# The last slot and the last units on VectorE: low codes, products, weighing and the closing sum, with the last four units in four PSUM banks

## The chip, the cores and the metric

One core of a Trainium2 chip. The metric is the device time in microseconds of one execution of the whole program; the time given for the kernel before is the median of 3 runs.

The engines are called by the names of the profile: PE (TensorE), ACT (ScalarE), DVE (VectorE), POOL (GpSimd), and SP, whose queue issues most DMAs.

## What is computed

16 images of 96x96 with 77 text tokens each become 16 x 113 = 1808 tokens of 192 features. One attention layer follows, and then a mixture-of-experts layer in which all 16 experts work on every token, each on a selection of half the features:

```python
pe = softmax(posembed @ pos_w + pos_b)
y = moe_mlp(hidden, sg_w, su_w, sd_w)                      # shared, 384 wide
for i in range(16):
    gate_feature = hidden * pe[i] @ gate_w + gate_b
    gate_weight, gate_idx = top_k(gate_feature, 96)        # of 192
    gate_weight = softmax(gate_weight)
    gathered = take_along_axis(hidden, gate_idx, axis=-1)
    y = y + moe_mlp(gathered * gate_weight, eg_w[i], eu_w[i], ed_w[i])
yn = (y - mean(y)) * rsqrt(var(y) + 1e-6) * ln_g + ln_b
return silu(yn @ m1_w + m1_b) @ m2_w + m2_b                # + hidden before the norm
# moe_mlp(x, g, u, d) = silu(x @ g) * (x @ u) @ d
```

## The kernel before, in words

**Tiles and slots.** The tokens are one rest tile of 16 and 14 tiles of 128. A tile's 16 experts go in 4 groups of 4; a group of a tile is a block, and every engine's program is a row of `slot`s, one per block, 57 in all (numbers 0 to `LAST` = 56). VectorE's slot is the top-k search (`max`, `max_index`, `match_replace`, lines 620 to 626), 12 rounds for each of 4 experts, and then the digits of the indices (lines 600 and 601).

**The gather.** It is done by matmuls, 8 tokens (an octet) at a time, 16 octets in a slot. An index is split into a high and a low digit. For octet o, `make_code` on PE (line 1144) writes two banks, `CODE_B` and `CODE_B + 1`, of 384 columns: where the digit is met, the value is 1, and elsewhere 0 or less. ACT's `code_out` (line 745) copies both with a Relu to `code`. `look` (line 1154) multiplies the high code with a table of the tokens' features into `LOOK_B`, one of two banks. ACT's `looked_up` (line 753) copies that to SBUF, and POOL multiplies it with the low code to `picked` (line 995). `put` (line 1164) sums `picked` for every 4 octets into the bank `XG_B`. ACT's `scale_out` (line 807) scales it with `einv` to `xs`, and POOL's `weigh` (line 963) multiplies it with the exponentials `ew` to `xw`. PE's `turn_x` (line 1173) transposes it, ACT's `turned_out` (line 719) copies it to `xwt`.

**The units.** A unit is one expert (or half of the shared layer) on one tile. `up` on PE (line 1207, 8 matmuls) writes gate and up features into the one bank `GU_B`. ACT's `activate` writes tanh of half the gate (line 793) and a copy of the bank (line 794). POOL's `hide` makes three products and sums (lines 930, 933, 936), and `down` (line 1227, 4 matmuls) adds into the bank `Y_B`. An `up` waits until ACT has read the unit before.

**The order.** It is written by hand in tables of steps, 16 steps to a slot, the same steps on all engines (`UNIT_SPOTS`, `GATE_SPOTS`, `TAIL_SPOTS`, `DOWN_LAG`, `TURN`, `FINAL_*`). In each step ACT, POOL and PE do the octet and then `step_work(step)`: a unit at its spot, its `down` 4 steps later, the turn of the block before at step 3, pieces of the next images' attention. ACT's `prepare(n + 1)` at step 8 of slot n waits for VectorE's search of the block n + 1, so that these engines run behind VectorE. Block 56's four units have the spots 5, 7, 9, 11 of the steps behind the last slot (`AFTER` and on), and the last tile's end follows.

**A tile's end.** ACT copies `Y_B` to `y` with its sum (line 815), takes the squares (line 822), POOL the mean and the power (lines 1002 to 1009), ACT normalises (line 825). PE turns it (line 1236), ACT scales and shifts (line 829), PE the first layer (line 1242), ACT adds the bias (line 835) and takes tanh of half (line 839), POOL a product and a sum (lines 1012, 1014), PE the second layer (line 1248), ACT halves it into `m2s` (line 844), POOL adds `resid` (line 1019) and issues the store to `out` (line 1021) from its own queue.

Of the kernel before, what the change touches and what calls it, by code (L numbers as in the profile page):

```python
# [189 lines left out]
GATE_AT = gate_steps()  # L190
TURN_AT = {OCT * (n + 1) + TURN: n for n in range(LAST + 1)}
FINAL_PE_AT, FINAL_ACT_AT, FINAL_POOL_AT = final_steps(FINAL_PE), final_steps(FINAL_ACT), final_steps(FINAL_POOL)

# [52 lines left out]
def build(nc, patches, txt, w_patch, b_patch, w_qk, scale, w_v, w_o, pos_t, w_pos, w_gate, b_gate, w_shared,  # L246
# [7 lines left out]
    with ExitStack() as ctx:  # L254
# [128 lines left out]
        m1_done, st1_ready, m2_done, fin_ready = sem("m1_done"), sem("st1_ready"), sem("m2_done"), sem("fin_ready")  # L383
        out_done = sem("out_done")

# [21 lines left out]
        with nc.Block() as block:  # L407

            @block.sync
            def _(sp):  # L410
# [127 lines left out]
                sp.wait_ge(late_in, LATE)  # L538
                sp.wait_ge(out_done, 16 * TILES + 16)

            @block.vector
            def _(dve):
# [99 lines left out]
                slots(slot)  # L642

            @block.scalar
            def _(act):
# [93 lines left out]
                def code_out(n, o):  # L739

                    act.wait_ge(code_done, OCT * n + o + 1)
                    if n or o >= 4:
                        act.wait_ge(picked_ready, OCT * n + o - 3)
                    w = experts_of(n) * TOP
                    nc.scalar.activation(code[:, o % 4, :, 0:w], ps[:, CODE_B:CODE_B + 2, 0:w], ACT.Relu).then_inc(code_ready, 1)  # L745

# [29 lines left out]
                def slot(t, g):  # L776
                    n = block_no(t, g)
                    for o in range(OCT):
                        looked_up(n, o)
# [107 lines left out]
                slots(slot)  # L887
                for step in range(AFTER, AFTER + 2 * OCT + 2):
                    step_work(step)

            @block.gpsimd
            def _(pool):
# [95 lines left out]
                def slot(t, g):  # L988
                    n = block_no(t, g)
                    w = slice(0, experts_of(n) * TOP)  # L990
                    for o in range(OCT):
                        pool.wait_ge(looked_out, OCT * n + o + 1)
# [43 lines left out]
                slots(slot)  # L1036
                for step in range(AFTER, AFTER + 2 * OCT + 2):
                    step_work(step)

            @block.tensor  # L1040
            def _(pe):
# [105 lines left out]
                def look(n, o):  # L1147
# [3 lines left out]
                    pe.wait_ge(code_ready, OCT * n + o + 1)  # L1151
                    if n or o >= 2:
                        pe.wait_ge(looked_out, OCT * n + o - 1)
# [3 lines left out]
                def put(n, r):  # L1157

                    if r == 0 and n:
                        pe.wait_ge(scaled, n)  # L1160
                    pe.wait_ge(picked_ready, OCT * n + QUADS * (r + 1))
                    w = slice(0, experts_of(n) * TOP)
# [12 lines left out]

                def up(tm, u, e, half):
                    rest_tile = tm == 0
# [13 lines left out]
                    pe.wait_ge(gu_out, GU_NTH["unit", tm, u] - 1)  # L1191
                    for a in range(2):
                        for c in range(2):
                            wide = REST if rest_tile and e is None else TILE
                            at = a * D + c * HALF
                            dst = ps[0:HALF, GU_B, (2 * a + c) * TILE:(2 * a + c) * TILE + wide]
                            if e is None:
# [13 lines left out]
                def down(tm, u, e, half):  # L1211
# [4 lines left out]
                    last_u = (REST_UNITS if rest_tile else UNITS) - 1  # L1216
                    many = PACK if e == "band" else 1
                    for x in range(many):
                        for c in range(2):
# [7 lines left out]
                            ins = nc.tensor.matmul(ps[0:REST if rest_tile else TILE, Y_B, 0:D], hid[:, u % 2, c, own], w,  # L1227
                                                   start=(u == 0 and x == 0 and c == 0), stop=(u == last_u and x == many - 1 and c == 1))
# [77 lines left out]
                slots(slot)  # L1306
                for step in range(AFTER, AFTER + 2 * OCT + 2):
                    step_work(step)

# [70 lines left out]
```

## Time and profile before

| | |
|---|---|
| median of 3 runs | 2670.26 us |
| lowest, highest | 2662.3, 2677.62 us |
| the profiled execution | 2661.93 us |
| its span | 2660.1 us |
| VectorE, PE, POOL, ACT busy | 94%, 85%, 67%, 64% of the span |
| mean granted TensorE clock | 0.906 |

The profile shows one execution, in microseconds from the start of the span. PE is TensorE's matmuls, PEld its weight loads. A granted clock of 1.00 is 2.4 GHz, of 0.50 is 1.2 GHz.

### The profile page before, as it was taken

The page shows a single profiled execution, that of the slowest core. Times are in us where ns is not written, and L with a number is a line of the kernel's source. Part 1 is how long each engine was busy: PE and PEld are TensorE (multiplying, and loading weights), DVE is VectorE, ACT ScalarE, POOL GpSimd, SP SyncE. Part 2 cuts the span into 40 slices and gives each one's busy share as a digit, 9 for nine tenths or more (in the row PEclk, how much of TensorE's full clock was granted, in tenths as well). Part 3 has the DMA queues.
Part 4 walks back from the last instruction along what each step waited for, and adds up shares of the span by engine and source line. Part 5 has one row for each costly group of instructions (what it writes and reads, how often), then busy time and mean ns, then how long its engine had stood idle before and what let it go on. Part 6 is the DMA issues. An engine that isn't in the chain of part 4 may idle for free.

```text
span 2660.1 us, 48026 instructions
## 1 busy us (share of the span) xinstructions
PE 2264.7 (85%) x11466; PEld 1232.5 (46%) x11466; DVE 2488.9 (94%) x13377; ACT 1703.8 (64%) x3995; POOL 1773.8 (67%) x2142
## 2 busy tenths in 40 slices
PE   4478998888889889898988988989899888897886
PEld 3345544444454454454544544445445443353444
DVE  3699799999999999999999999999999999999960
ACT  2243776767676667577675767667666666666664
POOL 1133878677677676677766777768677676676766
PEclk8587999999998989899898999899989898889877
DMA  2211222222222222122221222222122122221220
GB/s 61 54 31 39 52 53 59 49 55 51 46 59 53 51 53 52 49 53 52 52 52 44 58 45 55 56 49 62 45 54 50 40 58 52 52 53 45 49 49 16
DMA packets 124750, 133.67 MB, mean 50 GB/s; under 512 B 39931, under 2 KB 112598, under 8 KB 124462
## 3 DMA queue, kind: packets, MB, share of 16 engines
q1 hardware_dynamic: 122996, 127.82, 20.6%
q8 instruction: 95, 1.56, 0.2%
q0 software_dynamic: 928, 1.72, 0.2%
q14 instruction: 185, 1.52, 0.2%
q10 hardware_dynamic: 546, 1.06, 0.1%
HBM read 102.77 MB, written 27.87 MB: 49 GB/s over the span
## 4 chain that ended last, share of the span: by engine, by line
DVE 84%; PE 7%; DMA 3%; issue 2%; ACT 2%; POOL 1%; SPq 1%; ACTq 0%; POOLq 0%; DVEq 0%
DVE idx L624 30%; DVE keys L626 28%; DVE vals L620 24%; PE ps L1154 1%; PE ps L1227 1%; DMA looked_s<-in_mask_in 1%; DMA digit_d<-dcode 1%; DVE nmax L580 1%; SPq L465 1%; PE ps L1204 1%; DMA rows<-digit_d 1%; DVE ntop L596 1%; PE ps L1207 1%; DVE digits L601 0%; PE ps L1078 0%
## 5 line engine op out<-in xcount | busy, mean ns | idle before, releaser
L995 POOL TENSOR_TENSOR picked<-looked_s,code 128x384 f32<-128x384 f32 (+1 forms) x912 | 896.1, 991 | 479.0 <-ACT looked_s L753 477.2
L624 DVE FIND_INDEX8 idx<-vals,keys 128x8 uint16<-128x192 f32 x2712 | 939.8, 347 | 0.0
L753 ACT ACTIVATE looked_s<-ps 128x384 f32<-128x384 f32 (+1 forms) x912 | 447.8, 491 | 630.2 <-PE ps L1154 628.1
L620 DVE MAX8 vals<-keys 128x8 f32<-128x192 f32 x2712 | 820.3, 342 | 30.7 <-ACT keys L712 30.7
L626 DVE MATCH_REPLACE8 keys<-vals,keys 128x192 f32<-128x192 f32 x2486 | 839.9, 338 | 0.0
L1154 PE MATMUL ps<-code,table 128*128 128x384 f32 (+1 forms) x1824 | 832.5, 540 | 0.0
L745 ACT ACTIVATE code<-ps 128x768 f32<-128x768 f32 (+1 forms) x912 | 738.0, 809 | 59.2 <-PE ps L1144 52.0
L1144 PE MATMUL ps<-rows,codew 17*128 17x384 bf16 (+1 forms) x1824 | 317.8, 345 | 217.0 <-ACT code L745 155.5
L1144 PEld LDWEIGHTS ps<-rows,codew 17*128 17x128 bf16 x1824 | 86.6, 91 | 767.8 <-ACT code L745 416.4
L1154 PEld LDWEIGHTS ps<-code,table 128*128 128x128 f32 x1824 | 309.4, 202 | 201.1 <-issue 166.1
L1207 PE MATMUL ps<-xwt,wexp 96*96 96x128 f32 x1792 | 270.4, 298 | 37.4 <-ACT xwt L719 32.9
L1207 PEld LDWEIGHTS ps<-xwt,wexp 96*96 96x96 f32 x1792 | 219.5, 174 | 103.8 <-ACT xwt L719 46.6
L1164 PE MATMUL ps<-picked,place 128*32 128x384 f32 (+1 forms) x1824 | 217.3, 552 | 25.7 <-POOL picked L995 25.7
L930 POOL TENSOR_TENSOR prod_s<-gu_s 96x256 f32<-96x256 f32 x256 | 184.6, 721 | 80.8 <-ACT gu_s L794 79.4
L1227 PE MATMUL ps<-wdown,hid 96*128 96x192 f32 (+1 forms) x960 | 220.6, 357 | 1.9 <-POOL hid L936 1.8
L1122 PE MATMUL ps<-wgate,nt_gate 96*128 96x384 f32 x448 | 188.2, 546 | 14.6 <-DMA nt_gate<-normt_d 11.5
L933 POOL TENSOR_TENSOR turned_s<-prod_s,tanh_s 96x256 f32<-96x256 f32 x256 | 184.5, 721 | 20.1
L936 POOL TENSOR_TENSOR hid<-prod_s,turned_s 96x256 f32<-96x256 f32 x256 | 184.1, 719 | 20.0
L624 DVE MATCH_VALUE_LOAD idx<-vals,keys 128x8 f32 x2712 | 195.4, 72 | 0.0
L955 POOL TENSOR_TENSOR dcode<-dcode 128x768 bf16<-128x768 bf16 (+1 forms) x57 | 82.9, 1454 | 167.5 <-ACT dcode L727 167.5
L1227 PEld LDWEIGHTS ps<-wdown,hid 96*128 96x128 f32 (+1 forms) x960 | 159.1, 194 | 43.2 <-issue 27.9
L626 DVE MATCH_VALUE_LOAD keys<-vals,keys 128x8 f32 x2486 | 166.9, 67 | 0.0
(145 smaller groups left out, 2212.1 us busy)
## 6 DMA issues: line engine op xcount, KB each, us to landing
wexp<-in_w_exp SPq DMA_DIRECT2D x58, 576.0 KB, 4.4
wdown<-in_w_down SPq DMA_DIRECT2D x58, 576.0 KB, 4.4
digit_d<-dcode SPq DMA_DIRECT2D x56, 384.0 KB, 2.6
rows<-digit_d SPq DMA_DIRECT2D x224, 96.0 KB
table<-norm_d SPq DMA_DIRECT2D x448, 3.0 KB
patch<-in_patches SPq DMA_DIRECT2D x16, 108.0 KB, 4.9
tok_d<-h SPq DMA_DIRECT2D x16, 84.8 KB
norm_d<-hs SPq DMA_DIRECT2D x16, 84.8 KB
```

Source lines behind the costliest of these rows:

```text
L620: nc.vector.max(vals[:, par, e, at], from_keys[:, e, :]).then_inc(chain, 1)
L624: found = nc.vector.max_index(idx[:, par, e, at], vals[:, par, e, at], from_keys[:, e, :])
L626: nc.vector.match_replace(from_keys[:, e, :], vals[:, par, e, at], from_keys[:, e, :], NEG).then_inc(chain, 1)
L745: nc.scalar.activation(code[:, o % 4, :, 0:w], ps[:, CODE_B:CODE_B + 2, 0:w], ACT.Relu).then_inc(code_ready, 1)
L753: nc.scalar.activation(looked_s[:, o % 4, 0:w], ps[:, LOOK_B[o % 2], 0:w], ACT.Copy).then_inc(looked_out, 1)
L995: nc.gpsimd.tensor_tensor(picked[:, o % PICKS, w], looked_s[:, o % 4, w], code[:, o % 4, 1, w], ALU.mult).then_inc(picked_ready, 1)
L1122: ins = nc.tensor.matmul(ps[:, bank, 0:2 * D], nt_gate[0:HALF + k, k, :], wgate[0:HALF + k, k, GRP * g + 2 * pair:GRP * g + 2 * pair + 2, ...
L1144: ins = nc.tensor.matmul(ps[:, CODE_B + a, w], codew[at, :], rows[at, octet(o), w], start=True, stop=True)
L1154: ins = nc.tensor.matmul(ps[:, LOOK_B[o % 2], w], table[:, o, :], code[:, o % 4, 0, w], start=True, stop=True)
L1164: ins = nc.tensor.matmul(ps[32 * q:32 * (q + 1), XG_B, w], place[:, r, :], picked[:, (QUADS * r + q) % PICKS, w], start=(r == 0), stop=(r ...
L1207: ins = nc.tensor.matmul(dst, wexp[:, e // GRP % 2, e % GRP, at:at + HALF], xwt[:, e % GRP, :], start=True, stop=True)
L1227: ins = nc.tensor.matmul(ps[0:REST if rest_tile else TILE, Y_B, 0:D], hid[:, u % 2, c, own], w, start=(u == 0 and x == 0 and c == 0), stop ...
```

## The change

In the last slot and behind it VectorE, whose search is over, takes over work. The core of the diff (the added semaphores `code_low`, `picked_last`, `doubled`, `out_last` and some lines of the same kind left out):

```diff
+LAST_UNITS = [UNIT_AT[AFTER + spot] for spot in TAIL_SPOTS]
+LAST_BANKS = [GU_B, CODE_B, CODE_B + 1, LOOK_B[0]]
...
# sync
-                sp.wait_ge(out_done, 16 * TILES + 16)
+                sp.wait_ge(fin_ready, TILES + 1)
+                sp.dma_start(out[start(TILES):start(TILES) + TILE, :], fin[:]).then_inc(out_last, 16)
+                sp.wait_ge(out_done, 16 * TILES)
+                sp.wait_ge(out_last, 16)
...
# vector, behind slots(slot)
+                def low_codes(o):
+                    dve.wait_ge(code_done, OCT * LAST + o + 1)
+                    if o < 4:
+                        dve.wait_ge(picked_ready, OCT * LAST + o - 3)
+                    nc.vector.tensor_scalar(code[:, o % 4, 1, :], ps[:, CODE_B + 1, 0:COLS], 0.0, None, ALU.max).then_inc(code_low, 1)
+                def pick(o):
+                    dve.wait_ge(looked, OCT * LAST + o + 1)
+                    if o % QUADS == 0:
+                        dve.wait_ge(placed, QUADS * LAST + (o - PICKS) // QUADS + 1)
+                    dve.wait_ge(code_low, o + 1)
+                    nc.vector.tensor_tensor(picked[:, o % PICKS, :], ps[:, LOOK_B[o % 2], 0:COLS], code[:, o % 4, 1, :],
+                                            ALU.mult).then_inc(picked_last, 1)
+                def hide_last(j):
+                    u, bank = LAST_UNITS[j][1], LAST_BANKS[j]
+                    gu = ps[0:HALF, bank, :].rearrange("p (a c j) -> p a c j", a=2, c=2)
+                    place_of = (prod_s if j < 2 else turned_s)[:, j % 2]
+                    tanh_of = tanh_s[:, j] if j < 2 else gu_s[:, j - 2, 0]
+                    dve.wait_ge(gu_out, GU_NTH["unit", TILES, u])
+                    dve.wait_ge(hidden, units_before(TILES) + LAST_UNITS[0][1])
+                    for c in range(2):
+                        ins = nc.vector.scalar_tensor_tensor(place_of[:, c], tanh_of[:, c], 1.0, gu[:, 0, c], ALU.add, ALU.mult)
+                    ins.then_inc(doubled, 1)
+                    dve.wait_ge(doubled, j + 1)
+                    nc.vector.tensor_tensor(place_of, place_of, gu[:, 1], ALU.mult).then_inc(hidden, 1)
+                low_codes(0)
+                for o in range(OCT):
+                    if o + 1 < OCT:
+                        low_codes(o + 1)
+                    pick(o)
...
+                for e in range(GRP):
+                    ins = nc.vector.scalar_tensor_tensor(xw[:, e, :], ps[:, XG_B, e * TOP:(e + 1) * TOP], einv[:, LAST % 2, e:e + 1],
+                                                         ew[:, LAST % 2, e, :], ALU.mult, ALU.mult)
+                ins.then_inc(weighted, 1)
+                for j in range(len(LAST_UNITS)):
+                    hide_last(j)
+                dve.wait_ge(tanh_ready, TILES + 1)
+                nc.vector.scalar_tensor_tensor(st1[0:HALF], zt[:], 1.0, st1[0:HALF], ALU.add, ALU.mult).then_inc(st1_ready, 1)
...
+                nc.vector.scalar_tensor_tensor(fin[:], ps[:, MISC_B, 0:D], 0.5, resid[:], ALU.mult, ALU.add).then_inc(fin_ready, 1)
# scalar: in slot LAST no looked_up, code_out copies CODE_B only and waits for looked;
# behind slots(slot)
-                for step in range(AFTER, AFTER + 2 * OCT + 2):
-                    step_work(step)
+                activate(*UNIT_AT[AFTER - 1][0:3])
+                turned_out(LAST)
+                act.wait_ge(hidden, units_before(TILES) + LAST_UNITS[0][1])
+                for j, (tm, u, e, half) in enumerate(LAST_UNITS):
+                    gu = ps[0:HALF, LAST_BANKS[j], :].rearrange("p (a c j) -> p a c j", a=2, c=2)
+                    act.wait_ge(gate_up, units_before(tm) + u + 1)
+                    nc.scalar.activation(tanh_s[:, j] if j < 2 else gu_s[:, j - 2, 0], gu[:, 0], ACT.Tanh, scale=0.5).then_inc(gu_out, 1)
+                for what in ("y", "square", "norm", "zt", "st1"):
+                    final(TILES, what)
# gpsimd: in slot LAST no products, only step_work; behind slots(slot)
+                hide(*UNIT_AT[AFTER - 1][0:3])
+                for step in range(2):
+                    final(TILES, step)
# tensor, make_code
+                    if n == LAST and o:
+                        pe.wait_ge(code_low, o)
# tensor: look and put wait for picked_last in slot LAST; up takes a bank; down takes the source;
# behind slots(slot)
+                put(LAST, OCT // QUADS - 1)
+                for step in range(AFTER - DOWN_LAG, AFTER):
+                    if step in UNIT_AT:
+                        down(*UNIT_AT[step])
+                turn_x(LAST)
+                for unit, bank in zip(LAST_UNITS, LAST_BANKS):
+                    up(*unit, bank)
+                for unit in LAST_UNITS:
+                    down(*unit)
+                for step in range(3):
+                    final(TILES, step)
```

## Rows read from the trace of the kernel before

**Rows 1.** The page: the chain that ended last, shares of the span by engine

```profile
DVE 84%; PE 7%; DMA 3%; issue 2%; ACT 2%; POOL 1%; SPq 1%; ACTq 0%; POOLq 0%; DVEq 0%
```

**Rows 2.** Timeline of DVE, its last instruction: start us, us, what

```profile
2573.16 0.25 DVE L601 TENSOR_SCALAR digits<-idx 128x384 uint16<-128x384 uint16 x1
```

**Rows 3.** Busy time by stage: stretch, PE, PEld, DVE, ACT, POOL, granted clock, DMA

```profile
2591.00:2620.70 29.70, 27.30 (x146) 13.12 (x144) 0.00 (x0) 22.13 (x44) 25.89 (x31) 1.00 0.17 44
2620.70:2644.40 23.70, 15.98 (x68) 13.05 (x68) 0.00 (x0) 5.95 (x15) 13.98 (x19) 0.68 0.00 1
```

**Rows 4.** Groups of instructions from 2591 to 2623.1: busy us, mean ns, idle before

```profile
L995 POOL TENSOR_TENSOR picked<-looked_s,code 128x384 f32<-128x384 f32 x17 | 16.7, 992 | 2.3 <-ACT looked_s L753 2.3
L745 ACT ACTIVATE code<-ps 128x768 f32<-128x768 f32 x15 | 12.2, 812 | 1.2 <-POOL picked L995 1.1
```

**Rows 5.** Timeline of PE in the last slot, in brackets its idle time before

```profile
2593.29 0.85 PE L1164 MATMUL ps<-picked,place 128*32 128x384 f32 x8 [1.18 <-POOL picked L995]
...
2607.18 0.33 PE L1144 MATMUL ps<-rows,codew 17*128 17x384 bf16 x2 [0.17 <-ACT code L745]
...
2619.66 1.04 PE L1207 MATMUL ps<-xwt,wexp 96*96 96x128 f32 x8
2623.08 0.85 PE L1164 MATMUL ps<-picked,place 128*32 128x384 f32 x8 [2.38 <-POOL picked L995]
```

**Rows 6.** The chain of waits in order of time, around and behind the last slot

```profile
2598.61 0.57 PE ps L1173 x4
2599.18 0.65 PE ps L1227 x4
...
2601.71 0.49 ACT xwt L719
...
2626.41 1.06 PE ps L1173 x4
2627.47 1.28 PE ps L1227 x4
2628.75 1.72 PE ps L1207 x8
...
2639.42 0.03 ACT tanh_s L793
...
2640.36 0.73 POOL prod_s L930
...
2642.74 1.66 PE ps L1227 x4
...
2644.42 0.43 ACT y L815 x2
...
2652.40 0.72 POOL zt L1012
...
2655.72 0.34 ACT m2s L844
...
2656.12 0.59 POOL m2s L1019
```

**Rows 7.** Groups of DVE instructions of other shapes than the search: busy us, mean ns

```profile
L573 DVE TENSOR_SCALAR wgate<-gatew,pe_col 96x192 f32<-96x192 f32 x32 | 7.4, 309 | 0.0
...
L552 DVE TENSOR_TENSOR wqk<-wqk,looked_s 128x768 f32<-128x768 f32 x1 | 1.0, 958 | 3.1 <-DMA looked_s<-in_scale 3.1
...
L558 DVE TENSOR_REDUCE looked_s<-ps 16x1 f32<-16x192 f32 x1 | 0.3, 346 | 4.4 <-PE ps L1283 4.4
```

**Rows 8.** Busy time of PE in two stretches: us, busy, granted clock, DMA

```profile
2625.80:2639.20 13.40, 10.88 (x45) 0.50 0.01 1
2639.40:2642.80 3.40, 1.62 (x9) 0.98 0.00 0
```

**Rows 9.** DMA issues: queue, count, KB each, median us from issue to landing

```profile
digit_d<-dcode SPq DMA_DIRECT2D x56, 384.0 KB, 2.6
...
out<-m2s POOLq DMA_DIRECT2D x14, 96.0 KB, 3.3
```

More of the change, by code:

```diff
@@ new lines, in _ @@
+                ins.then_inc(weighted, 1)
[3 more added lines that the diff above has]
+                nc.vector.scalar_tensor_tensor(st1[0:HALF], zt[:], 1.0, st1[0:HALF], ALU.add, ALU.mult).then_inc(st1_ready, 1)
+                dve.wait_ge(m2_done, TILES + 1)
+                dve.wait_ge(resid_in, 16 * TILES + 16)
+                dve.wait_ge(out_done, 16 * TILES)
+                nc.vector.scalar_tensor_tensor(fin[:], ps[:, MISC_B, 0:D], 0.5, resid[:], ALU.mult, ALU.add).then_inc(fin_ready, 1)
@@ L741, in code_out @@
                     act.wait_ge(code_done, OCT * n + o + 1)
-                    if n or o >= 4:
+                    if n == LAST:
+                        act.wait_ge(looked, OCT * n + o - 3)
+                    elif n or o >= 4:
                         act.wait_ge(picked_ready, OCT * n + o - 3)
                     w = experts_of(n) * TOP
-                    nc.scalar.activation(code[:, o % 4, :, 0:w], ps[:, CODE_B:CODE_B + 2, 0:w], ACT.Relu).then_inc(code_ready, 1)
+                    if n < LAST:
+                        nc.scalar.activation(code[:, o % 4, :, 0:w], ps[:, CODE_B:CODE_B + 2, 0:w], ACT.Relu).then_inc(code_ready, 1)
+                    else:
+                        nc.scalar.activation(code[:, o % 4, 0, :], ps[:, CODE_B, 0:COLS], ACT.Relu).then_inc(code_ready, 1)
                 def looked_up(n, o):
@@ L778, in slot @@
                     for o in range(OCT):
-                        looked_up(n, o)
+                        if n < LAST:
+                            looked_up(n, o)
                         if o + 2 < OCT:
@@ L991, in slot @@
                     for o in range(OCT):
+                        if n == LAST:
+                            step_work(OCT * n + o)
+                            continue
                         pool.wait_ge(looked_out, OCT * n + o + 1)
@@ L1036, in _ @@
                 slots(slot)
-                for step in range(AFTER, AFTER + 2 * OCT + 2):
-                    step_work(step)
+                hide(*UNIT_AT[AFTER - 1][0:3])
+                for step in range(2):
+                    final(TILES, step)
             @block.tensor
@@ L1151, in look @@
                     pe.wait_ge(code_ready, OCT * n + o + 1)
-                    if n or o >= 2:
+                    if n == LAST and o >= 2:
+                        pe.wait_ge(picked_last, o - 1)
+                    elif n or o >= 2:
                         pe.wait_ge(looked_out, OCT * n + o - 1)
@@ L1160, in put @@
                         pe.wait_ge(scaled, n)
-                    pe.wait_ge(picked_ready, OCT * n + QUADS * (r + 1))
+                    if n == LAST:
+                        pe.wait_ge(picked_last, QUADS * (r + 1))
+                    else:
+                        pe.wait_ge(picked_ready, OCT * n + QUADS * (r + 1))
                     w = slice(0, experts_of(n) * TOP)
@@ L1174, in turn_x, with up @@
                     ins.then_inc(x_turned, 1)
-                def up(tm, u, e, half):
+                def up(tm, u, e, half, bank=GU_B):
                     rest_tile = tm == 0
@@ L1190, in up @@
                         pe.wait_ge(weights_in[e // GRP % 2], 32 * expert_load(tm, e // GRP) + 32)
-                    pe.wait_ge(gu_out, GU_NTH["unit", tm, u] - 1)
+                    if bank == GU_B:
+                        pe.wait_ge(gu_out, GU_NTH["unit", tm, u] - 1)
                     for a in range(2):
@@ L1195, in up @@
                             at = a * D + c * HALF
-                            dst = ps[0:HALF, GU_B, (2 * a + c) * TILE:(2 * a + c) * TILE + wide]
+                            dst = ps[0:HALF, bank, (2 * a + c) * TILE:(2 * a + c) * TILE + wide]
                             if e is None:
@@ L1217, in down @@
                     many = PACK if e == "band" else 1
+                    source = hid[:, u % 2]
+                    if (tm, u, e, half) in LAST_UNITS:
+                        j = LAST_UNITS.index((tm, u, e, half))
+                        source = (prod_s if j < 2 else turned_s)[:, j % 2]
                     for x in range(many):
@@ L1226, in down @@
                             own = slice(x * REST, (x + 1) * REST) if rest_tile else slice(0, TILE)
-                            ins = nc.tensor.matmul(ps[0:REST if rest_tile else TILE, Y_B, 0:D], hid[:, u % 2, c, own], w,
+                            ins = nc.tensor.matmul(ps[0:REST if rest_tile else TILE, Y_B, 0:D], source[:, c, own], w,
                                                    start=(u == 0 and x == 0 and c == 0), stop=(u == last_u and x == many - 1 and c == 1))
@@ L1306, in _ @@
                 slots(slot)
-                for step in range(AFTER, AFTER + 2 * OCT + 2):
-                    step_work(step)
+                put(LAST, OCT // QUADS - 1)
[9 more added lines that the diff above has]
+                    final(TILES, step)
 def kernel(**inputs):
```

6 lines of the change are left out of this document (5 added, 1 removed).

## The prediction

> **What bounds the kernel now.** I began with the chain of waits over the whole span [rows 1]: 84% of it is VectorE, the top-k search. The change touches no instruction of that search, so only what comes after it can move. VectorE's last instruction starts at 2573.16 us [rows 2] and is over at 2573.4; the span ends at 2660.1. In these 86.7 us VectorE does nothing. It is the time in which the other four engines work off the last two slots, the last four units and the last tile's end.
>
> Next I cut that time by the engines' busy table [rows 3]. The last slot's 16 octets take from 2591.0 to 2620.7: PE 27.3 of 29.7 us, POOL 25.9, ACT 22.1. So PE is nearly full there, and its granted clock is at the high level. From 2620.7 to 2644.4 comes a chain with little overlap (PE 16.0 of 23.7, mean clock 0.68), and behind it the last tile's normalisation, two small layers and the store.
>
> PE's own order of time in the slot [rows 5] says how the two limits share it. PE stands 1.18 us before 2593.29, for the previous slot's last product on POOL, which the change leaves alone. In octets without other work it waits 0.17 us for ACT's code. The last unit's four blocks of matmuls end at 2620.70 (2619.66 plus 1.04), and then PE stands 2.38 us for POOL's last product. POOL is the late one at the end of the slot, PE in most of it.
>
> **The slot, part by part.** Removed: 16 products on POOL of 0.99 us and as many copies on ACT; ACT's code copy falls from 768 to 384 columns, from 0.81 us [rows 4]. Added: 32 VectorE instructions of 384 elements with one operand in PSUM. No row has this shape. Bounds: 0.31 us (192 elements in SBUF) and 0.96 us (768) [rows 7]. The straight line between them is 1.13 ns per element, so 384 make 0.53; a reduction of 192 out of PSUM takes 0.35 where SBUF takes 0.31, so 0.04 more: 0.57 us, and I take that since it lies between near rows. Two per octet make 1.1 us, against 29.7/16 = 1.86 us that an octet takes and 27.3/16 = 1.7 that PE needs. VectorE is hidden by PE then. The new wait is on make_code, for the low codes of the octet before; behind it in PE's queue stand the put, the turn, the units. In an octet with nothing else the low copy queues behind the product, so PE would wait about 0.2 us for it, as it now waits 0.17 for ACT: nothing gained, nothing lost. Of PE's 2.4 idle us in the slot, 1.18 stay; of the other 1.2 I take **0.9** as gained. Call A the end of the slot's last unit matmuls: 2620.7 before, 2619.8 after.
>
> **From A to the turn.** Before, the turn starts at 2626.41 [rows 6], A+5.7: last product, put, scaling on ACT, weighing on POOL, which also has a unit's three products ahead of it. After, put runs at A, and VectorE weighs in four instructions of 96 elements (0.20+0.04 each, 1.0 in all): ready at A+1.9. What is late next is the down of the last slot's unit, which now stands ahead of the turn in PE's order: ACT 0.9, POOL's three steps 2.4 (2640.36 to 2642.74), down 0.65 at the high clock: A+4.0. Gain **1.7**. POOL's and ACT's other work has room to spare.
>
> **Turn to the first unit.** Before 2.34 us (2626.41 to 2628.75), with a down in between. After: turn 0.57 and ACT's copy 0.53 with its hand-overs, 1.15 at the high clock, or 1.65 with the turn at 1.06. Gain **1.2 or 0.7**.
>
> **The four units.** Before, one bank: each waits for ACT's two reads, 2628.75 to 2639.40, 10.65 us. After, four banks and no wait: 4 x 1.04 = 4.2 us at the high clock [rows 5], 4 x 1.72 = 6.9 at the low one [rows 6]. Gain **6.5 or 3.8**.
>
> **Last unit to the last down.** Before, 2639.40 to 2644.40, 5.0 us: ACT, three POOL steps, a down of 1.66. After: ACT's tanh 0.4, two VectorE instructions of 128 elements (0.24 each, with PSUM's 0.04 0.28) and one of 256 (0.42): 1.5 us. But three downs stand before the fourth: 1.95 plus 0.8 at the high clock, 2.75; 3.84 plus 1.66 at the low one, 5.5. Gain **2.2, or a loss of 0.5**.
>
> **The end.** Two POOL steps of 0.72 and their hand-over (1.6) become one VectorE instruction of 256 elements (0.4, and hand-overs): **1.1**. ACT's 0.34 and POOL's 0.59 out of PSUM [rows 6] become one of 192 (0.35 to 0.4): **0.6**. The store moves from POOL's queue to SP's, which has nothing left ahead of it; the old way takes 3.4 us from the sum's end at 2656.71 to the span's end. POOL's stores land 3.3 us after issue, while SP's store of four times the bytes lands in 2.6 [rows 9], and POOL needs 0.3 us before it issues: I take **1.0** as gained, bounds 0 and 1.4. By the Trainium skill ("DMA: Bandwidth & Descriptors", Latency and other measured facts) the first byte comes after about 0.6 us from SP and 1 us from GpSimd, an estimated gain of 0.4 from that page's figures, so the whole would be 0.6 less; no run here shows that split.
>
> **Sum.** At the high clock throughout: 0.9+1.7+1.2+6.5+2.2+2.7 = 15.2. At the low one from the turn on: 0.9+1.7+0.7+3.8-0.5+2.7 = 9.3. So the clock in the unit stage is the term that decides. Before, it fell at about 2625.8, after PE had stood for 2.4 us and again ahead of the turn, and came back at about 2639.3, after a stretch in which PE worked 10.9 of 13.4 us [rows 8]. After the change PE still stands about 1.8 us (A+1.5 to A+3.3) and 0.6 us, less than before, and then works without a break for 7 to 12 us. So I expect a fall in some executions and a return within the units: about half the difference, **12.3 us** gained. The Trainium skill ("TensorE: Matmul & The Clock Gate", Part 1) says that the slow clock is the default and activity releases it; the trace agrees, in so far as the clock came back while PE worked through the units.
>
> The profiled execution took 2661.93 us, 1.8 more than its span of 2660.1; it would become 2649.6. It is the lowest but for 0.4 us of the three runs shown, 8.3 below their median of 2670.26. The gain doesn't depend on what makes runs differ, so I take it off the median: **2658.0 us**, 0.46% less.
>
> **The rivals.**
> 1. The clock stays high: 15.2 us, 2655.1. For it: PE's pauses shrink. Against: one of 1.8 us is left, and pauses of that kind brought the clock down before.
> 2. The clock falls and stays low through units and downs: 9.3 us, 2661.0. For it: before, the low level lasted 13 us. Against: in those, PE stood 2.5 us between the units, and here it wouldn't.
> 3. VectorE becomes the slot's bound, since ACT, PE and VectorE now all work on PSUM. It decides from 1.7/2 = 0.86 us an instruction; at price p it costs 16 x (2p-1.7), which eats the whole gain at p = 1.24. At 1.4 us it costs 17.6, and the kernel takes 2675.6, slower than before. Against: 768 elements take only 0.96 us.
> 4. The slot's end doesn't come sooner and the units aren't what the end waits for, because the down of the slot's last unit on POOL holds the turn longer than counted: then steps of the slot and to the turn are lost, 2.6 us, and 9.7 remain: 2660.6.
>
> **How the numbers follow.** Under 0.5%, 13.35 us, a measurement of this kernel can't well tell from no change. Chances: forecast 0.45, rival 1 0.25, rival 2 0.17, rival 3 0.05 (slower in most of it), rival 4 0.08. Faster by over 0.5%: nearly all of rival 1 and over a third of the forecast, whose 12.3 is 1 us short of the bound: 0.42. Slower by over 0.5% only in the worst of rival 3, or by the spread of runs: 0.04. Same: 0.54. The range reaches from 15.2 and a low draw of runs (2647) to 9.3 with a median that lies 5 us high (2667); the runs shown spread by 15 us.
>
> **What would show it.** VectorE instructions of 384 elements at about 0.57 us, and PE idle under 2 us in the last slot, so that VectorE's search ends 46 us before A. Turn about 4.0 us after A; four units with no gap, 4.2 to 6.9 us; the last down's end at 2632 to 2638 on the old scale; fewer than 2.7 us from the store's issue to the end. The forecast is wrong if octets take 2 us or more with PE waiting for VectorE, if the down ahead of the turn comes later than A+5, or if the time before 2591 changes.

## The result, and the profile after

| | before | after |
|---|---|---|
| median | 2670.26 us | 2651.57 us (5 runs, 2648.44 to 2657.78) |
| ratio | | 0.9934, 95% interval 0.9916 to 0.9953 |
| the profiled execution | 2661.93 us | 2657.78 us |
| its span | 2660.1 us | 2655.9 us |

The change makes the kernel 18.7 us faster by the medians, and by 12.5 to 22.4 us within the interval. Forecast were 2658.0 us and a gain of 12.3 us; the measured median lies in the range given (2647 to 2667). The ratio is not that of the two medians (0.9930); by it the gain is 17.6 us. Two later groups of runs gave the same kernel ratios of 0.9947 (0.9929 to 0.9965) and 0.9952 (0.9930 to 0.9973), 14.1 and 12.8 us, so 18.7 us is the high end, and the three groups together say some 15 us.

The busy table by stage, of the profile after: stretch and its length, PE, PEld, DVE, ACT, POOL, granted clock, DMA share and GB/s. It answers to [rows 3].

```profile
2600.10:2628.40 28.30, 27.07 (x150) 13.30 (x150) 15.43 (x30) 11.39 (x27) 12.45 (x17) 1.00 0.18 46
2628.40:2643.40 15.00, 12.59 (x69) 11.08 (x68) 4.58 (x16) 2.97 (x7) 2.16 (x3) 0.77 0.00 1
```

The first line is the last slot. POOL is busy for 12.5 us instead of 25.9, ACT for 11.4 instead of 22.1, and VectorE has 15.4. PE does the same 27 us of work, and the slot gets only 1.4 us shorter. The second line runs from the slot's last up to the last down: 15.0 us instead of 23.7, for about as many matmuls (69 in the trace, 68 before).

What PE waited for in the last slot (us in total, times, longest), before:

```profile
PE ps L1164 <- POOL picked L995: 1.2, 1, 1.2
PE ps L1144 <- ACT code L745: 0.9, 4, 0.4
```

and after:

```profile
PE ps L1245 <- POOL picked L1068: 0.8, 1, 0.8
```

The four waits for ACT's code are gone, none for VectorE's low codes came in their place, and the wait for the previous slot's last product is 0.3 us shorter.

What VectorE's new instructions cost, in the groups of DVE behind its search (busy us, mean ns of one, idle before). They answer to [rows 7].

```profile
L663 DVE TENSOR_TENSOR picked<-ps,code 128x384 f32<-128x384 f32 x16 | 8.9, 558 | 12.9 <-PE ps L1232 12.5
L655 DVE TENSOR_SCALAR code<-ps 128x384 f32<-128x384 f32 x16 | 8.8, 549 | 13.6 <-PE ps L1220 13.6
L689 DVE SCALAR_TENSOR_TENSOR xw<-ps,einv,ew 128x96 f32<-128x96 f32 x4 | 1.0, 311 | 1.1 <-PE ps L1245 1.1
L675 DVE SCALAR_TENSOR_TENSOR prod_s<-tanh_s,ps 96x128 f32<-96x128 f32 x4 | 1.0, 279 | 6.8 <-ACT tanh_s L957 6.8
...
L678 DVE TENSOR_TENSOR prod_s<-prod_s,ps 96x256 f32<-96x256 f32 x2 | 0.8, 418 | 0.1
...
L699 DVE SCALAR_TENSOR_TENSOR m2s<-ps,resid 128x192 f32<-128x192 f32 x1 | 0.4, 358 | 1.8 <-PE ps L1334 1.8
```

The 384 elements take 0.55 to 0.56 us, where the line between two other shapes had given 0.57. VectorE waits for PE before 12 of its 16 products, not PE for VectorE.

The timeline of PE from the previous slot's last put to the units, idle time in brackets. It answers to [rows 5].

```profile
2602.04 0.85 PE L1245 MATMUL ps<-picked,place 128*32 128x384 f32 x8 [0.84 <-POOL picked L1068]
...
2627.39 1.04 PE L1289 MATMUL ps<-xwt,wexp 96*96 96x128 f32 x8
2628.36 0.85 PE L1245 MATMUL ps<-picked,place 128*32 128x384 f32 x8
2629.14 0.92 PE L1313 MATMUL ps<-wdown,hid 96*128 96x192 f32 x4
2631.78 0.92 PE L1313 MATMUL ps<-wdown,hid 96*128 96x192 f32 x4 [1.72 <-POOL hid L1006]
```

The put that stood 2.38 us before it ran now follows the up at once; in its place the down of the slot's last unit stands 1.72 us for POOL. The chain of waits from there on, which answers to [rows 6]:

```profile
2632.70 0.45 PE ps L1254 x4
...
2633.17 0.60 ACT xwt L776
...
2633.82 6.96 PE ps L1289 x32
2640.78 2.62 PE ps L1313 x16
...
2643.42 0.43 ACT y L878 x2
...
2651.11 0.43 DVE st L695
...
2651.68 1.63 PE ps L1334 x4
...
2653.33 0.36 DVE m2s L699
```

All 32 matmuls of the four ups are one piece now, and all 16 of the downs another.

**Where the 4.2 us between the two spans hide 13.** The two profiled executions don't begin this part at the same time: VectorE's search ended at 2573.4 before and at 2585.1 after. The waits of DVE, before and after, show where that is from (us in total, times, longest):

```profile
DVE vals L620 <- ACT keys L712: 30.7, 3, 16.0
```

```profile
DVE vals L626 <- ACT keys L769: 41.8, 3, 27.1
```

The 11.1 us more are in the longest of these waits. It ended 303.8 us into the span before and 312.1 after, where the change touches nothing, and the search behind it took 3.3 us more. In later profiles of the changed kernel that wait was 19.8 and 23.3 us, and the search ended at 2578.3 and 2579.9. Of the kernel before there is one profile, so these rows alone don't show that the wait has the same spread there. The medians speak for it: less the 1.8 us outside the span and less the time behind the search (86.7 and 70.8 us in the two profiles), they put the search's end at about 2581.8 before and 2579.0 after, an estimate. So I compare stretches, cut at the same events in each trace. In the table, "first look" is the first matmul of line 1154 (before) of the last slot, A the end of its last up, "ups" the last four, all in us, with the mean granted clock of the ups; the last column is their sum, without the stretch ahead of the first look.

| kernel | search's end to first look | slot, to A | A to turn | turn to ups | ups (clock) | to last down's end | to last sum's end | to span's end | sum from first look |
|---|---|---|---|---|---|---|---|---|---|
| before | 17.6 | 29.67 | 5.71 | 2.14 | 10.84 (0.51) | 5.00 | 12.32 | 3.39 | 69.1 |
| after | 15.0 | 28.31 | 4.10 | 1.29 | 6.96 (0.52) | 2.60 | 10.31 | 2.21 | 55.8 |
| after_again | 15.9 | 28.30 | 4.10 | 1.28 | 5.40 (0.68) | 2.60 | 10.56 | 2.21 | 54.5 |
| after_third | 19.3 | 27.40 | 4.10 | 1.28 | 5.40 (0.68) | 2.60 | 10.56 | 2.16 | 53.5 |
| turn_first | 15.0 | 28.30 | 1.99 | 1.30 | 3.73 (1.00) | 3.25 | 10.55 | 2.16 | 51.3 |
| turn_first_again | 17.4 | 28.41 | 1.99 | 1.30 | 3.73 (1.00) | 3.25 | 10.55 | 2.20 | 51.4 |
| warm | 15.9 | 28.31 | 4.70 | 1.28 | 3.73 (1.00) | 2.62 | 10.54 | 2.20 | 53.4 |
| slot_before | 17.7 | 29.64 | 5.42 | 1.29 | 3.73 (1.00) | 2.61 | 10.54 | 2.21 | 55.4 |
| slot_only | 17.4 | 28.41 | 4.39 | 1.30 | 10.68 (0.52) | 5.00 | 12.32 | 3.41 | 65.5 |
| one_bank | 15.1 | 28.31 | 4.10 | 1.28 | 12.45 (0.50) | 4.83 | 10.55 | 2.21 | 63.7 |
| end_before | 17.4 | 28.40 | 4.11 | 1.28 | 5.40 (0.68) | 2.60 | 12.33 | 2.21 | 56.3 |
| store_pool | 15.3 | 28.31 | 4.11 | 1.28 | 6.72 (0.54) | 2.61 | 10.32 | 3.38 | 56.7 |
| one_more | 15.8 | 30.74 | 4.10 | 1.29 | 7.07 (0.52) | 2.59 | 10.31 | 2.20 | 58.3 |
| two_more | 17.6 | 37.86 | 4.72 | 1.74 | 5.59 (0.66) | 2.60 | 10.56 | 2.24 | 65.3 |

From the first look on, the change saves 13.3, 14.6 and 15.6 us in its three profiles. Some 0.9 us of the 15.6 are only moved: in after_third PE came to the slot late (19.3 us), found POOL's product ready, and so its slot has no wait of 0.84 us. The stretch ahead of it, where PE works through the end of the slot before at a clock that differs from execution to execution, varies between 15.0 and 19.3 us and is no part of the gain.

### The profile page after: what moved, and what is told of

It reads as the page before. It is cut to its first block, busy times and chain, and to the rows that moved or that the text cites. A ratio compares the mean times of both kernels' runs of the same rounds, so it can differ in the third digit from the quotient of the medians.

```text
span 2655.9 us, 48030 instructions
## 1 busy us (share of the span) xinstructions
PE 2278.8 (86%) x11466; PEld 1235.3 (47%) x11466; DVE 2513.5 (95%) x13427; ACT 1690.0 (64%) x3970; POOL 1747.4 (66%) x2109
## 4 chain that ended last, share of the span: by engine, by line
DVE 85%; PE 7%; DMA 3%; issue 2%; ACT 1%; SPq 1%; POOL 1%; ACTq 0%; POOLq 0%
DVE idx L630 30%; DVE keys L632 29%; DVE vals L626 24%; PE ps L1232 1%; DMA rows<-digit_d 1%; DMA digit_d<-dcode 1%; DMA looked_s<-in_mask_in 1%; PE ps L1313 1%; DVE nmax L586 1%; PE ps L1286 1%; SPq L468 1%; DVE ntop L602 1%; PE ps L1220 1%; PE ps L1289 0%; DVE digits L607 0%
## 5 line engine op out<-in xcount | busy, mean ns | idle before, releaser
L1068 POOL TENSOR_TENSOR picked<-looked_s,code 128x384 f32<-128x384 f32 (+1 forms) x896 | 880.8, 991 | 498.9 <-ACT looked_s L815 497.2
L815 ACT ACTIVATE looked_s<-ps 128x384 f32<-128x384 f32 (+1 forms) x896 | 440.0, 491 | 648.9 <-PE ps L1232 647.1
L805 ACT ACTIVATE code<-ps 128x768 f32<-128x768 f32 (+1 forms) x896 | 725.1, 809 | 57.5 <-PE ps L1220 53.5
L1289 PE MATMUL ps<-xwt,wexp 96*96 96x128 f32 x1792 | 265.0, 294 | 35.9 <-ACT xwt L776 33.6
L1196 PE MATMUL ps<-wgate,nt_gate 96*128 96x384 f32 x448 | 197.8, 569 | 14.7 <-DMA nt_gate<-normt_d 11.5
L1006 POOL TENSOR_TENSOR hid<-prod_s,turned_s 96x256 f32<-96x256 f32 x252 | 182.0, 722 | 19.8
L1003 POOL TENSOR_TENSOR turned_s<-prod_s,tanh_s 96x256 f32<-96x256 f32 x252 | 181.9, 722 | 19.8
```

Source lines behind the costliest of these rows:

```text
L815: nc.scalar.activation(looked_s[:, o % 4, 0:w], ps[:, LOOK_B[o % 2], 0:w], ACT.Copy).then_inc(looked_out, 1)
L1196: ins = nc.tensor.matmul(ps[:, bank, 0:2 * D], nt_gate[0:HALF + k, k, :], wgate[0:HALF + k, k, GRP * g + 2 * pair:GRP * g + 2 * pair + 2, ...
L1289: ins = nc.tensor.matmul(dst, wexp[:, e // GRP % 2, e % GRP, at:at + HALF], xwt[:, e % GRP, :], start=True, stop=True)
```

## The experiments

Theory: PE paces the last slot, so moving work off POOL and ACT gives little there; the gain lies behind it, in the four banks, the shorter steps of VectorE and the end. Main rival: the gain is POOL's relief in the slot.

The kernels slot_only, one_bank, end_before, store_pool, one_more and two_more were each run once, and the 12 runs of after_third alone spread over 27 us, so for these six I go by the stretches of the traces and not by the times.

**after_again** is the changed kernel itself, once more.

> The changed kernel itself, as the yardstick of this group. Both theories: its time against the kernel before lies at 0.9916 to 0.9953. From the end of the search on VectorE to the end of the span its profile had 70.7 us, against 86.7 before. If part of that is the TensorE clock ahead of the last slot (15.0 us from the search's end to the slot's first look, against 17.6), this stretch varies between profiles by some 2 us, while the stretches with PE waits are the same within 0.3 us.

Measured: 2657.58 us median of 7 runs, before 2667.98 (17 runs), ratio 0.9947 (0.9929 to 0.9965). The stretches are the same to 0.01 us, but for the ups (5.40 instead of 6.96, at a mean clock of 0.68 instead of 0.52), the one ahead of the first look and 0.25 us of clock in the end. Behind A the clock is the only thing that changes between executions of one kernel.

**slot_before.** The last slot as before the change, the rest changed.

```diff
-                low_codes(0)
-                for o in range(OCT):
-                    if o + 1 < OCT:
-                        low_codes(o + 1)
-                    pick(o)
# ACT: looked_up(n, o) and both codes in slot LAST too; POOL: its product too;
# PE: no wait for code_low, looked_out and picked_ready in place of picked_last
```

> Only the last slot is as before the change: POOL makes its products, ACT copies both codes and what was looked up; the weighing on VectorE, the four banks and the end stay changed. My theory: PE sets the slot's pace, so the slot's first look to the end of its last up is 29.7 us again instead of 28.3; then the put waits 2.4 us for POOL's last product, and POOL's three steps for the slot's unit come behind it, so the turn starts 6 us after the last up instead of 4.1. In all 3.3 us longer from the search's end than the changed kernel, 74. Rival (most of the gain of 16 us comes from taking work off POOL in the slot): 8 us longer or more.

Measured: ratio 0.9960 (0.9937 to 0.9983). The slot takes 29.64 us, the kernel before's to 0.03. PE's timeline behind it:

```profile
2630.98 0.85 PE L1224 MATMUL ps<-picked,place 128*32 128x384 f32 x8 [2.38 <-POOL picked L1054]
2631.76 0.92 PE L1292 MATMUL ps<-wdown,hid 96*128 96x192 f32 x4
2633.27 0.92 PE L1292 MATMUL ps<-wdown,hid 96*128 96x192 f32 x4 [0.59 <-POOL hid L995]
2634.02 0.60 PE L1233 MATMUL ps<-ident,xw 128*96 128x128 f32 x4
2635.31 3.73 PE L1268 MATMUL ps<-xwt,wexp 96*96 96x128 f32 x32 [0.68 <-ACT xwt L771]
```

The 2.38 us ahead of the put are back, and the turn starts at A+5.4. Slot and turn together are 1.3 + 1.3 = 2.7 us longer than in the changed kernel (forecast 3.3). The rival's 8 us are ruled out. The times, 0.9960 beside 0.9947 for the changed kernel, have overlapping intervals. One thing came otherwise: with these longer pauses the clock stayed at the high level through the ups, and that hides the loss in the sum (55.4 us).

**slot_only.** The other way round: the slot changed, all behind it as before.

```diff
-LAST_UNITS = [UNIT_AT[AFTER + spot] for spot in TAIL_SPOTS]
-LAST_BANKS = [GU_B, CODE_B, CODE_B + 1, LOOK_B[0]]
+LAST_UNITS = []
+LAST_BANKS = []
# VectorE ends behind its 16 products, the store is on POOL's queue; ACT, POOL and PE as before behind the slot:
+                for step in range(AFTER, AFTER + 2 * OCT + 2):
+                    step_work(step)
```

> The part of the change in the slot alone (low codes and products on VectorE); the weighing, the units in one bank with POOL's steps, the end and the store as before. My theory: the slot takes 28.3 us instead of 29.7; POOL has no product before the slot's last unit, so the turn starts sooner than 5.7 us after the last up, at 4.8 (put, scaling, and POOL's weighing behind its unit's three steps); ups, downs, end and store take the 10.8, 5.0, 12.3 and 3.4 us of before. 2 to 3 us less than before from the slot's first look on. Rival (the slot part is most of the gain): 8 us less or more.

Measured: 65.5 us from the first look on, 3.6 less than before: 1.3 in the slot, 1.3 to the turn, 0.8 behind it where the turn ran at the high clock, 0.2 in the ups. That is above the forecast of 2 to 3, because the turn started at A+4.4 (forecast 4.8) and ran at the high clock, which the forecast didn't count. Its chain of waits shows the old order at work, an up, then two reads by ACT, then the next:

```profile
2634.96 2.03 PE ps L1263 x8
2637.02 0.38 ACT tanh_s L838
2637.39 0.49 ACT gu_s L839
...
2637.93 2.02 PE ps L1263 x8
```

So of the 13.3 to 15.6 us, some 3 to 4 come from the work taken off in the slot (3.6 here, 2.7 in slot_before) and 10 to 12 from what was changed behind it.

**one_bank.** The units' steps stay on VectorE, but all in one bank.

```diff
-LAST_BANKS = [GU_B, CODE_B, CODE_B + 1, LOOK_B[0]]
+LAST_BANKS = [GU_B, GU_B, GU_B, GU_B]
...
                 for unit, bank in zip(LAST_UNITS, LAST_BANKS):
+                    if unit != LAST_UNITS[0]:
+                        pe.wait_ge(hidden, units_before(TILES) + unit[1])
                     up(*unit, bank)
```

> The last four units go through the one bank, so that each up waits until VectorE has read the one before; all else as changed. My theory: ups, tanh on ACT and VectorE's three instructions come one behind the other: 1.0 to 1.7 for the up and 1.45 for the rest, 2.5 to 3.1 us a unit, so from the first up to the last up's end 9 to 11 us instead of 7.0, and only one down is left behind the last (1.7 instead of 2.6 us after it, from 1.45 us on): 1.5 to 4 us longer. Rival (moving the work from POOL to VectorE gave the units' gain and the banks nothing): 0.5 us longer at most.

```profile
2626.36 2.02 PE L1289 MATMUL ps<-xwt,wexp 96*96 96x128 f32 x8 [0.68 <-ACT xwt L776]
2629.88 2.02 PE L1289 MATMUL ps<-xwt,wexp 96*96 96x128 f32 x8 [1.49 <-DVE prod_s L678]
```

12.45 us for the ups, and 4.83 behind them: 7.7 us more than in the changed kernel's slowest tail (17.28 against 9.56). The forecast was 1.5 to 4: it counted one down behind the last up, while the edit leaves all four there, and it did not count on the clock, which stayed low from the first up to the last down (PE worked 12.9 of these 17.3 us, standing 1.4 to 1.5 us ahead of three of the four ups). With the ups at the low clock in both kernels (0.50 and 0.52), the four banks make them 6.96 us instead of 12.45. With one bank VectorE's steps give nothing against the kernel before (17.28 against 15.84), so the gain needs the banks. Whether the banks would do as well with the steps left on ACT and POOL was not run.

**end_before.** The last activation and sum as before, on ACT and POOL.

```diff
-                nc.vector.scalar_tensor_tensor(st1[0:HALF], zt[:], 1.0, st1[0:HALF], ALU.add, ALU.mult).then_inc(st1_ready, 1)
-                nc.vector.scalar_tensor_tensor(fin[:], ps[:, MISC_B, 0:D], 0.5, resid[:], ALU.mult, ALU.add).then_inc(fin_ready, 1)
+                nc.gpsimd.tensor_tensor(fin[:], m2s[:], resid[:], ALU.add).then_inc(fin_ready, 1)
# ACT does its step "out" and POOL its step 2 again
```

> The last activation and the sum out of PSUM are done as before by ACT and POOL; the store stays on the sync engine's queue. My theory: from the start of y to the end of the last sum 12.3 us instead of 10.3, less what the clock gives: 1.7 to 2.0 us longer. Rival: within 0.3 us, as these steps are hidden.

Measured: 12.33 us for that stretch, against 10.56 at the same clock in the units: 1.8 us. POOL's timeline has the three instructions that VectorE's two replace (with ACT's copy of 0.33 us):

```profile
2644.38 0.72 POOL L1079 TENSOR_TENSOR zt<-zt,st 96x256 f32<-96x256 f32 x1 [5.51 <-ACT zt L896]
2645.17 0.72 POOL L1081 TENSOR_TENSOR st<-zt,st 96x256 f32<-96x256 f32 x1
2648.10 0.59 POOL L1109 TENSOR_TENSOR m2s<-m2s,resid 128x192 f32<-128x192 f32 x1 [2.21 <-ACT m2s L901]
```

**store_pool.** The last store from POOL's queue.

```diff
-                sp.dma_start(out[start(TILES):start(TILES) + TILE, :], fin[:]).then_inc(out_last, 16)
+                pool.wait_ge(fin_ready, TILES + 1)
+                pool.dma_start(out[start(TILES):start(TILES) + TILE, :], fin[:]).then_inc(out_last, 16)
```

> The last store is issued from POOL's queue as before, behind the sum on VectorE. My theory: 3.3 to 3.4 us from the sum's end to the end of the span, instead of 2.2, so 1.1 longer. Rival (the time is the write's, whoever issues it): the same 2.2 us.

Measured: 3.38 us instead of 2.21, 1.2 longer. The rival falls. The two issues, of this kernel and of the changed one:

```profile
2655.12 0.64 POOL L1112 DMA_DIRECT2D out<-m2s  x1 [8.12 <-DVE m2s L697]
```

```profile
2653.76 0.37 SPq L543 DMA_DIRECT2D out<-m2s  x1
```

POOL begins 0.30 us after the sum, SP 0.07; POOL's issue takes 0.64, SP's 0.37; from there to the span's end it is 2.44 and 1.77 us. So 0.2, 0.3 and 0.7 us make up the 1.2.

**warm.** PE's pauses ahead of the units are filled with matmuls whose result nobody reads.

```diff
+                for k in range(4):
+                    nc.tensor.matmul(ps[:, LOOK_B[1], 0:COLS], table[:, 0, :], code[:, 0, 0, :], start=True, stop=True)
                 down(*UNIT_AT[AFTER - 1])
                 turn_x(LAST)
+                nc.tensor.matmul(ps[:, LOOK_B[1], 0:COLS], table[:, 0, :], code[:, 0, 0, :], start=True, stop=True)
```

> Four matmuls of 384 columns without use are put into PE's pause ahead of the last slot's down, and one behind the turn; nothing else changes. If the level of the clock in the units is set by PE's pauses ahead of them, the ups run at the high level, 4.2 us for 32 matmuls instead of 7.0, and the tail is up to 2.7 us shorter. Rival (the clock falls and rises whatever PE does there, or the two levels cost nothing): the ups take 7.0 us as before, and the tail is longer by what the added matmuls overrun, 0 to 0.3 us.

```profile
2626.20 2.75 PE L1396 MATMUL ps<-code,table 128*128 128x384 f32 x8
2628.78 0.82 PE L1313 MATMUL ps<-wdown,hid 96*128 96x192 f32 x4
2629.43 0.60 PE L1254 MATMUL ps<-ident,xw 128*96 128x128 f32 x4
2629.87 0.81 PE L1399 MATMUL ps<-code,table 128*128 128x384 f32 x2
2630.71 3.73 PE L1289 MATMUL ps<-xwt,wexp 96*96 96x128 f32 x32
```

The ups run at the high level, 3.73 us. The added four take 2.6 us where the pause was 1.7 (each stands twice in the row, x8), so the turn starts 0.6 us later (forecast was an overrun of at most 0.3), and from A to the last down 1.1 and 2.6 us remain (12.3 against 13.4 and 15.0) as gain in the tail. By the time, 0.9948 (0.9930 to 0.9967), it can't be told from the changed kernel.

**turn_first.** The turn goes ahead of the down that waits for POOL.

```diff
-                for step in range(AFTER - DOWN_LAG, AFTER):
-                    if step in UNIT_AT:
-                        down(*UNIT_AT[step])
+                down(*UNIT_AT[AFTER - 3])
                 turn_x(LAST)
                 for unit, bank in zip(LAST_UNITS, LAST_BANKS):
                     up(*unit, bank)
+                down(*UNIT_AT[AFTER - 1])
```

> The turn of the last block stands ahead of the down of the last slot's unit; the down comes behind the four ups. My theory: that down, for which PE stands 1.7 us, holds the turn, so the turn starts about 2.0 us after the end of the slot's last up instead of 4.1; the four ups follow 1.3 us later, and PE's pauses shrink to 0.4 and 0.7 us, so that the clock stays at the high level and the ups take 4.2 us instead of 7.0. The tail gets shorter by 2.1 us less the down (0.65) that moves behind the ups, and by up to 2.8 more from the clock: 1.5 to 4.2 us. Rival (the turn waits for the weighing on VectorE and not for the down): nothing changes by more than 0.5 us.

> The same kernel as in the run turn_first, timed in more rounds beside the changed kernel. Its first profile had 66.3 us from the search's end to the span's end against 70.3 and 70.8 of the changed kernel, but its search ended late (2590.5). If what is before the search's end differs between executions by chance, the medians show 4 us between this and the changed kernel, 0.9925 to 0.994 of the kernel before; the stretches with PE waits come out again within 0.1 us. Rival (the late search is this order's doing): the search ends late again and the times are the changed kernel's.

> The changed kernel as it is, again, for the comparison with the turn moved ahead. Search's end to span's end 70 to 71 us; time 0.993 to 0.995 of the kernel before.

The chain of waits of turn_first:

```profile
2633.82 0.83 PE ps L1245 x8
...
2634.67 1.00 DVE xw L689 x4
...
2635.81 0.63 PE ps L1254 x4
...
2636.46 0.60 ACT xwt L776
...
2637.11 3.73 PE ps L1289 x32
2640.84 3.27 PE ps L1313 x20
```

POOL is off the chain. The turn starts at A+1.99, as forecast, the downs behind the ups take 0.65 us more for the one that moved there, the ups ran at the high clock in both profiles, and the sum from the first look is 51.3 and 51.4 us, 2.1 to 4.5 less than the changed kernel's three. Of that the order itself gives 1.5 (2.11 less 0.65), and the rest is the clock: 1.7 or 3.2 in the ups (less the 0.9 us that after_third's slot was short of). The late search of the first profile (2590.5) is not this order's doing: the second had 2570.6. Times: 0.9940 (0.9916 to 0.9964) beside 0.9947 for the changed kernel in the first group; 0.9925 (0.9901 to 0.9949) beside 0.9952 (0.9930 to 0.9973) in the second. Both point the same way, but the intervals overlap; the traces carry the verdict. after_third itself missed its forecasts by little: 72.8 us from the search's end where 70 to 71 were expected, for the stretch ahead of the slot (19.3 us), and a ratio of 0.9952 where 0.993 to 0.995 was expected.

**one_more and two_more.** VectorE does one or two products more in each octet.

```diff
                     dve.wait_ge(code_low, o + 1)
+                    nc.vector.tensor_tensor(score[:, 0].rearrange("p h j -> p (h j)")[:, 0:COLS], ps[0:TOK, LOOK_B[o % 2], 0:COLS], code[0:TOK, o % 4, 1, :],
+                                            ALU.mult).then_inc(extra, 1)
...
# also a wait before each added product for the one before it, and once, ahead of
# the slot, for the last attention step, whose tile `score` takes the result
```

> VectorE does one more product of 384 columns (into a tile that nobody reads) in each octet of the last slot, ahead of the real one. VectorE then works 1.5 us an octet, in which PE needs 1.7. If PE sets the pace, the slot's 28.3 us grow only in octets without units, where the low codes come 0.47 us later: 7 of them, by 3 us at most. Rival (VectorE is at its limit in the slot): 16 x 0.47, 7.5 us longer.

> Two more products of 384 columns on VectorE in each octet of the last slot. VectorE then works some 2.0 us an octet against PE's 1.7, so by my theory it now sets the pace: 16 x 2.0 is 32 to 34 us for the slot instead of 28.3, against 30.7 with one more. Rival (the first added product already met VectorE's limit, and each costs the same): 33.2 us, 2.4 for each; a slot under 31.5 us would say that VectorE had still room.

With one more the slot takes 30.74 us, 2.4 longer, within the 3 us of the theory and far from 7.5; PE waits 2.7 us for VectorE's low codes, in six places. With two it takes 37.86. PE's timeline of that kernel:

```profile
2617.41 0.34 PE L1230 MATMUL ps<-rows,codew 17*128 17x384 bf16 x2 [0.35 <-DVE code L656]
2617.68 0.91 PE L1242 MATMUL ps<-code,table 128*128 128x384 f32 x2
2619.40 0.34 PE L1230 MATMUL ps<-rows,codew 17*128 17x384 bf16 x2 [0.81 <-DVE code L656]
2619.66 0.91 PE L1242 MATMUL ps<-code,table 128*128 128x384 f32 x2
2621.38 0.39 PE L1230 MATMUL ps<-rows,codew 17*128 17x384 bf16 x2 [0.81 <-DVE code L656]
2621.70 2.02 PE L1299 MATMUL ps<-xwt,wexp 96*96 96x128 f32 x8
```

Octets follow each other by 1.98 us (2617.41, 2619.40, 2621.38), and PE stands 0.81 us in each: VectorE sets the pace, as forecast. Why 37.9 and not 32 to 34: PE waits 6.4 us for the low codes, and its clock falls after these pauses (the up in the last line takes 2.02 us instead of 1.11, the slot's mean clock is 0.91), which makes its own work 30.6 us instead of 27.1. So VectorE comes to pace most of the slot somewhere between 1.5 and 2.0 us an octet, and here crossing that cost more than VectorE's own time.

## Why the prediction was right, point by point

Its form was right: PE paces the slot, the clock in the units decides the size, the end gives a few us. In the changed kernel's own profile, from the first look on, 13.3 us were gained. The 12.3 of the forecast is no sum of one case but the middle between the clock high throughout (15.2) and low throughout (9.3). What came was the mixed case, low in the ups and high in turn and downs; the prediction's own terms give 12.5 for it (0.9+1.7+1.2+3.8+2.2+2.7), so that the middle lay so near it was in part luck. In the two repeats the clock came back within the ups (5.40 us), as the forecast had it. Of its signs of being wrong one came, that the time before 2591 changes: the first look at 2600.1 instead of 2591.0; that is the search's late end, treated above.

- **Slot**: 0.9 forecast, 1.36 measured, a repeat 1.37. The waits show where: the 0.9 us for ACT's code are gone, where the prediction let VectorE's low codes take their place ("nothing gained, nothing lost"), and the 1.18 us that it let stay became 0.84. In slot_before, with ACT's full copies back, both waits are back (0.9 and 1.2). In after_third the slot took 27.40, without the second wait.
- **VectorE's price**: 0.57 forecast, 0.55 to 0.56. The 0.04 that it added for PSUM does not show: 256 elements took 0.42 with an operand in PSUM (line 678) and 0.42 from SBUF (line 695), though by different operations. The weighing's four of 96 elements took 0.31 each where 0.24 was forecast, yet 1.0 in all as forecast, since they overlap. The limit of 0.86 us an instruction for rival 3 stands in the right place (one_more is 0.7 to 0.8 us per real instruction, two_more about 1.0), its size was too small: at 1.0 us it gives 4.8, and two_more's slot is 9.6 longer, 3.5 of it PE's work at the lower clock.
- **A to the turn**: A+4.0 forecast, A+4.10. The down of the slot's unit was named as what is late next; turn_first shows it by taking it away. Rival 4, that it holds the turn longer, is out.
- **Turn to the first unit**: gain 1.2 at the high clock, measured 2.14 to 1.29, 0.85. The prediction read the first up's start from the chain (2628.75); by PE's timeline it is 2628.55, so this stretch was 2.14 and the ups 10.84 instead of 10.65.
- **Ups**: 4.2 at the high clock, 6.9 at the low. Measured 3.73 (0.93 a unit in one piece, where 1.04 is the row of a unit by itself) and 6.96. Of the six profiles that keep this order and these banks and leave the slot's pace about as it is, three have 5.40 and three 6.7 to 7.1: rival 1 never came in these, and rival 2 only in the ups, since the downs always took 2.6 us, at the high level.
- **Last unit to last down**: 2.75 forecast, 2.60.
- **End**: 1.1 and 0.6 forecast, 1.8 in end_before; the store 1.0, measured 1.2.

The distance from 12.3 to the measured 18.7 us is mostly not in the sum: the traces give 13.3 to 15.6, and the rest, 3 to 5, is the first group's draw of runs. By their ratios the three groups have 17.6, 14.1 and 12.8 us. By the bound of 0.5% the three come out on either side, which is what chances of 0.42 and 0.54 said.

One reason that I gave doesn't hold as I gave it. I tied the clock to PE's pauses ahead of the units: shorter pauses, higher clock. It stayed high with filled pauses (warm) and with pauses of 0.36 and 0.68 us (both turn_first). But slot_before, with pauses of 2.38, 0.59 and 0.68 us, kept it high too, and the changed kernel, with 1.72 and 0.68, never did. So filling or shortening the pauses went with a high clock in three profiles of three, yet which pause makes it fall in a given execution these runs don't tell. With one profile of slot_before, it stays open.

## What to carry to other kernels

Here three engines served a fourth that was already 92% busy, and relief for the three gave part of what the fourth idled, 1.4 of 29.7 us. Behind the last loop, where little overlaps, free PSUM banks turned a chain of matmul, read, matmul into one block: 10.8 to 5.4 or 7.0 us, and without them the faster engine alone gave nothing. Then look at what a queue's order puts ahead of the critical instruction: one down moved behind the ups brought the turn 2.1 us forward and cost 0.65 later, net as much as the slot got shorter by its whole rewrite, and the clock stayed high as well.

## What the runs showed of the hardware that I had not expected

- VectorE instructions with an operand in PSUM took 0.28 us for 128 elements, 0.36 for 192, 0.42 for 256, 0.55 to 0.56 for 384; 256 elements from SBUF alone (line 695) took 0.42 as well. Those of line 689, 96 elements with a scalar per partition (`einv`), took 0.31, more than the 128. Back to back, the 384 start every 0.47 us.
- The same 96 KB store ends 2.2 us after its data when SP issues it and 3.4 when POOL does.
- The same four ups took 3.73, 5.40 or 6.7 to 7.1 us by the granted clock. Between two profiles of the changed kernel (6.96 and 5.40) every other stretch from the first look to the span's end was equal to 0.01 us, but for 0.25 in the end, which is the clock as well.
- The search ended between 2570.6 and 2590.5 us in the profiles of all runs, and both ends are of one kernel, turn_first. One wait of VectorE for keys, some 300 us into the span, was 16.3 us in the one profile and 26.3 in the other, and its end lay 8.9 us apart. The other 11.0 us arose behind it, where the trace shows no wait of VectorE until the search is over.
